# A four-layer graph network on one core: block sums loaded before the last run is stored, counting by quarters, and 32-row products in the update

## The reference

```python
edge_index = jnp.stack([src, dst])                 # 50,000 edges
h = jnp.maximum(_layernorm(x, axis=-1), 0.0)
x = x + _L0_gnn_ref(h, edge_index, edge_weight, w, slw)      # sum at dst
h = jnp.maximum(_layernorm(x, axis=-1), 0.0)
x = x + _L1_gnn_ref(h, edge_index, edge_attr_2, w1)          # sum at src
h = jnp.maximum(_layernorm(x, axis=-1), 0.0)
x = x + _L2_gnn_ref(h, edge_index, edge_attr_8, ...)         # both directions
h = jnp.maximum(_layernorm(x, axis=-1), 0.0)
x = x + _L3_gnn_ref(h, edge_attr_8, node_vec1, ...)
# in _L3_gnn_ref, after agg = segment_sum(m, row):
u = jnp.einsum('ni,nh,ihk->nk', node_features, agg, W_upd_tp) * norm_upd_tp
u = jax.nn.silu(u)
return node_features + (u @ W_upd_lin) * norm_lin
```

## Time and profile before

| what | value |
|---|---|
| times of three runs | 5128.19, 5087.6, 5112.34 us |
| median | 5112.34 us |
| the profiled execution: time, span | 5145.52 us, 5143.8 us |
| mean granted TensorE clock | 0.688 of full speed |
| busy PE, DVE, POOL, ACT | 44%, 54%, 53%, 23% of the span |

### The profile page before, as it was taken

The page is one execution under the profiler, slowest core; times in us unless marked ns, Lnnn a source line. Parts: engine busy times, 40 slices in busy tenths (PEclk is TensorE's granted clock), DMA queues, the critical chain, the costliest instruction groups (busy, mean ns, idle before and its releaser), DMA issues.

```text
span 5143.8 us, 30784 instructions
## 1 busy us (share of the span) xinstructions
PE 2267.1 (44%) x8710; PEld 1601.6 (31%) x8710; DVE 2773.4 (54%) x4101; ACT 1188.9 (23%) x2921; POOL 2750.7 (53%) x2767
## 2 busy tenths in 40 slices
PE   1110036767622100344444226666641455444998
PEld 0000025555511000233333114444431344333444
DVE  8200944545500006355555856767675566565998
ACT  0000012222201102233333323333332223222011
POOL 4777345555577771555555044555523555543787
PEclk6555567878755555677777657777775777777999
DMA  5000112222310012122223412222242222223010
GB/s 148 9 8 8 28 61 84 94 76 94 84 22 22 13 24 84 51 87 80 79 80 81 124 51 77 85 84 85 84 114 79 82 82 82 82 82 92 22 36 29
DMA packets 192782, 345.70 MB, mean 67 GB/s; under 512 B 81018, under 2 KB 159466, under 8 KB 164067
## 3 DMA queue, kind: packets, MB, share of 16 engines
q1 hardware_dynamic: 106128, 290.26, 15.4%
q0 software_dynamic: 81344, 21.38, 5.9%
q10 hardware_dynamic: 5140, 32.09, 1.6%
HBM read 66.26 MB, written 277.24 MB: 67 GB/s over the span
## 4 chain that ended last, share of the span: by engine, by line
another core or an unknown queue 28%; DVE 25%; PE 19%; issue 18%; ACT 3%; POOL 3%; SPq 2%; DMA 1%; DVEq 0%; POOLq 0%
DVE natS L1197 7%; PE psK L570 6%; PE psX L719 4%; PE psK L566 4%; DVE work L1177 3%; PE psX L545 2%; ACT work L829 1%; POOL natD L511 1%; DVE natD L1197 1%; DVE work L1197 1%; DVE h L1087 1%; SPq L430 1%; DVE psX L1084 1%; PE psX L643 1%
## 5 line engine op out<-in xcount | busy, mean ns | idle before, releaser
L487 POOL DMA_INDIRECT rows<-table,rec x1760 | 1666.9, 947 | 1932.5 <-DMA table<-h 508.7
L1197 DVE SCALAR_TENSOR_TENSOR natS<-natS,keep,psK 128x256 f32<-128x256 f32 x1320 | 634.4, 481 | 639.6 <-remote 468.9
L570 PE MATMUL psK<-work 128*128 128x256 f32 x2640 | 787.0, 451 | 425.5 <-issue 196.9
L570 PEld LDWEIGHTS psK<-work 128*128 128x128 f32 x2640 | 595.0, 233 | 576.4 <-issue 385.9
L829 ACT ACTIVATE work<-iota,rec 128x128 f32<-128x128 f32 x1760 | 536.3, 391 | 793.3 <-remote 611.3
L1177 DVE TENSOR_TENSOR work<-at_hi,psX 128x2048 f32<-128x2048 f32 x220 | 502.4, 2284 | 4.2 <-issue 0.4
L469 POOL DMA_INDIRECT edges_by_dst<-natD,pos x391 | 393.3, 1006 | 181.3 <-issue 126.9
L469 POOL DMA_INDIRECT edges_by_src<-natS,pos x391 | 393.1, 1005 | 130.2 <-issue 130.2
L545 PE MATMUL psX<-keep,ident 128*128 128x256 f32 x1080 | 331.9, 431 | 254.3 <-issue 251.0
L566 PE MATMUL psK<-work 128*128 128x128 f32 x1760 | 300.1, 350 | 136.4 <-DVE work L1177 111.0
L719 PE MATMUL psX<-natD,work 128*128 128x512 f32 x784 | 348.3, 596 | 23.6 <-DMA work<-scan_by_column 15.5
(11 more groups left out here) (158 smaller groups left out, 2590.6 us busy)
## 6 DMA issues: line engine op xcount, KB each, us to landing
scan<-natS SPq DMA_DIRECT2D x110, 1024.0 KB
scan_by_column<-natS SPq DMA_DIRECT2D x55, 1024.0 KB
scan<-natD SPq DMA_DIRECT2D x28, 1024.0 KB
rows<-table,rec POOLq DMA_INDIRECT x1760
scan<-work SPq DMA_DIRECT2D x27, 1024.0 KB
table<-h ACTq DMA_DIRECT2D x28, 896.0 KB, 3.6
work<-scan SPq DMA_DIRECT2D x147, 128.0 KB, 2.1
rec<-edges_by_dst SPq DMA_DIRECT2D x110, 84.0 KB
```

The source lines that it names most:

```text
L487: pool.indirect_dma_start(out=rows[k][:, u * D:(u + 1) * D], out_offset=None, in_=table.ap(), in_offset=bass.IndirectOffsetOnAxis(ap=rec[k ...
L570: k = nc.tensor.matmul(psK[:, o:o + BW], lo, spread[par][:, o:o + BW], start=True, stop=True)
L1197: V.scalar_tensor_tensor(acc[par][:, t * BW:(t + 1) * BW], was, keep[s][:, q * G + t:q * G + t + 1], psK[:, t * BW:(t + 1) * BW], ALU.mult ...
```

## The change

There are three edits. First, on SP the loads of the block sums no longer come behind the last `keep_run` of a layer. SP waits for PE's last sum (`summed`) and for the stores of the groups before the last, loads the first chunk, and stores the last group between the first chunk's loads and the second's. Tiles move so that nothing is overwritten: `sq2` goes to `work`, the even accumulator of layer 3 too, and ACT waits for the last two stores before the update. Second, `sort` makes the masks in four quarters of 13, each with its own increment of `in_block`, and `count` waits quarter by quarter; `keys(1)` moves behind the first sort's masks, and `nxt` behind the positions. Third, the update's two products of a step take 32 rows each, those of their two nodes.

```diff
--- before.py
+++ after.py
@@ -180,7 +180,7 @@
         W4 = W1
         uA = prod[:, 0:CW]
         assert nat_at <= NAT * FD, nat_at
-        sq2 = natS[:, 0:CW]
+        sq2 = work[:, 7168:7168 + CW]
         small2 = natS[:, 4096:4096 + 4 * CH]
 
         outer, outerT = prod[:, 1024:1536], prod[:, 1536:2048]
@@ -191,7 +191,8 @@
         tD = natD[:, 2048:2048 + CW]
         halves = [prod[:, i * 512:(i + 1) * 512] for i in range(4)]
 
-        accs = [[prod, work[:, 6144:8192]]] + [[natS[:, i * 2048:(i + 1) * 2048] for i in range(2)]] * 3
+        in_natS = [natS[:, i * 2048:(i + 1) * 2048] for i in range(2)]
+        accs = [[prod, work[:, 6144:8192]], in_natS, in_natS, [work[:, 7168:9216], in_natS[1]]]
 
         psK = ctx.enter_context(nc.psum_tensor("psK", [P, 2048], f32))
         psX = ctx.enter_context(nc.psum_tensor("psX", [P, 2048], f32))
@@ -411,12 +412,12 @@
                         fetch(g + RING)
                         if g:
                             keep_run(g - 1)
-                    for g in range(GROUPS - RING - 1, GROUPS):
-                        keep_run(g)
-                    for g in (GROUPS - 2, GROUPS - 1):
-                        sp.wait_ge(run_out[g % 2], kept_runs(l, g))
-
-                    for c in range(NCH):
+                    def runs_out(g):
+                        for q in (g - 1, g):
+                            sp.wait_ge(run_out[q % 2], kept_runs(l, q))
+
+                    def block_sums(c):
+
                         if l < 3:
                             if c >= 2:
                                 sp.wait_ge(nd[l + 1]["took" if l else "mixed"], c - 1)
@@ -430,6 +431,17 @@
                             t = sp.value_load(last[s][0:1, bass.ds(j + c * PER, 1)], min_val=0, max_val=T - 1)
                             sp.dma_start(to[:, bass.ds(j * BW, BW)], whole.ap()[:, bass.ds(t * BW, BW)])\
                                 .then_inc(signal, 16)
+
+                    for g in range(GROUPS - RING - 1, GROUPS - 1):
+                        keep_run(g)
+
+
+                    sp.wait_ge(e["summed"], GROUPS * G)
+                    for c in range(NCH):
+                        if c == 1:
+                            keep_run(GROUPS - 1)
+                        runs_out(max(GROUPS - 2, (T - 1 - (NB - PER * (c + 1))) // G))
+                        block_sums(c)
 
         @block.gpsimd
         def _(pool):
@@ -520,11 +532,12 @@
 
             def count(s):
 
-                pe.wait_ge(in_block, s + 1)
                 if s:
                     pe.wait_ge(kept, 1)
                 for w, ps in ((allones, psX), (lower, psK)):
                     for b in range(4):
+                        if w is allones:
+                            pe.wait_ge(in_block, 4 * s + (b + 1))
                         for v in range(VS):
                             k = nc.tensor.matmul(v3(ps[:, b * 512:b * 512 + JW], GS), w[:, :],
                                                  OH[:, b * JB:(b + 1) * JB, v * GS:(v + 1) * GS],
@@ -715,7 +728,7 @@
 
                     for j in range(2):
                         b, m = q // 2, 2 * (q % 2) + j
-                        two = slice(0, P)
+                        two = slice(32 * m, 32 * m + 32)
                         k = nc.tensor.matmul(psQ[q % 2][:, j * 512:(j + 1) * 512], sums_in[c % 2][two, b * P:(b + 1) * P],
                                              W4[two, m * 512:(m + 1) * 512], start=True, stop=True)
                     k.then_inc(up["prod"], 1)
@@ -942,6 +955,9 @@
                 if not first:
                     store_out(c - 1)
 
+
+            for g in (GROUPS - 2, GROUPS - 1):
+                act.wait_ge(run_out[g % 2], kept_runs(3, g))
             step(0, True)
             for c in range(1, NCH):
                 step(c, False)
@@ -1009,11 +1025,18 @@
 
             def sort(s):
 
-                for j in range(NBS):
-                    own.did(V.tensor_scalar(OH[:, j, :], keyb[s], float(j), None, ALU.is_equal))
-                own.settle()
-                V.tensor_tensor(OH[:, :, ET:EC], OH[:, :, ET:EC],
-                                padmask[:, None, :].to_broadcast([P, NBS, 2]), ALU.mult).then_inc(in_block, 1)
+                for b in range(4):
+                    own_rows = slice(b * JB, (b + 1) * JB)
+                    for j in range(b * JB, (b + 1) * JB):
+                        own.did(V.tensor_scalar(OH[:, j, :], keyb[s], float(j), None, ALU.is_equal))
+                    own.settle()
+                    V.tensor_tensor(OH[:, own_rows, ET:EC], OH[:, own_rows, ET:EC],
+                                    padmask[:, None, :].to_broadcast([P, JB, 2]), ALU.mult).then_inc(in_block, 1)
+                if s == 0:
+
+                    keys(1)
+                    V.sem_inc(unstaged, 1)
+                    V.sem_inc(copied, 1)
                 A, B, C, I = tiny
                 E4 = before_g.rearrange("p (b j g) -> p b j g", b=4, g=GS)
                 all4 = psX[:, :].rearrange("p (b c) -> p b c", c=512)[:, :, 0:JW]\
@@ -1054,8 +1077,6 @@
                     hit = OH[:, :, v * GS:(v + 1) * GS].rearrange("p (b j) g -> p b j g", b=4)
                     now, nxt = [pre[(v + i) % 2].rearrange("p b (j g) -> p b j g", g=GS) for i in range(2)]
                     own.did(V.tensor_tensor(value.rearrange("p (b j g) -> p b j g", b=4, g=GS), hit, now, ALU.mult))
-                    if v < VS - 1:
-                        own.did(V.tensor_tensor(nxt, hit, now, ALU.add))
                     own.settle()
                     with nc.allow_low_precision(reason="one whole number below 2**24 and zeros"):
                         own.did(V.tensor_reduce(posi[0], value.rearrange("p (j g) -> p g j", g=GS), AX.X, ALU.add))
@@ -1065,6 +1086,9 @@
                     own.settle()
                     V.scalar_tensor_tensor(pos[s][:, v * GS:(v + 1) * GS], posi[1], float(T), posi[2],
                                            ALU.mult, ALU.add).then_inc(places[s], 1)
+                    if v < VS - 1:
+                        own.did(V.tensor_tensor(nxt, hit, now, ALU.add))
+                        own.settle()
 
                 dve.wait_ge(masks, MASKS)
                 dve.wait_ge(firstT, 2 * s + 1)
@@ -1296,9 +1320,6 @@
             dve.wait_ge(cleared, CLEARED)
             dve.wait_ge(ids_in, IDS)
             keys(0)
-            keys(1)
-            V.sem_inc(unstaged, 1)
-            V.sem_inc(copied, 1)
             sort(0)
             sort(1)
             dve.wait_ge(small_in, SMALL)
```

## The result

The changed kernel takes 5054.99 us (median of 9), the kernel before beside it 5119.98 (median of 9): a ratio of 0.988, 95% interval 0.9855 to 0.991. By the ratio that is 60 us less, by the two medians 65. The profiled execution of the changed kernel took 5054.01 us (span 5052.3), close to its median, while that of before, 5145.52, was 25 us over its own; so stages are compared by marks in the two traces, and the whole by the ratio and the medians.

What follows compares the result with a forecast made beforehand. No engine reached 55% busy, so each stage had its own limit. First sort -11.8, second sort -48, block sums -13.5 and 32-row products -24 summed to -97 us: 5112 to 5015, range 4970 to 5085.

Steps and rivals of the forecast that it cites:

- signs of being wrong: First gather staying over 650, or the update's granted clock at 0.6 or less with a chunk over 54 us.
- the pace: While POOL scatters, every engine gets one instruction per about 1.4 us; a product with its weight load takes 2.8.
- The start: First sort: masks in quarters, second keys and `nxt` moved; first scatter near 45.7, -11.8 us.
- The second sort: PE starts after 13 masks instead of 52; -48 us beyond the earlier first scatter, 60 in all.
- The count of products: Second sort: DVE's 156.87 us for the 56 products with `lower` equals 56 x 2.80.
- Rival (E): Second sort: some products run before POOL's scatters fill what paces them; 35 us more gain, 4979 us, chance 0.07.
- The block sums: Between layers and before the update: sooner loads give -3 and -4 behind layers 1 and 2, -6.5 before the update.
- Behind layer 0: Block-sum loads may start 6 to 8 us sooner, but `place(1)` ends no earlier: 0, bounds -6 and +6.
- 32-row products: Update: a step takes 1.13 us, DVE bounds a chunk at 49.8 us instead of 54.41; -24 us.
- I take 4 us off: Update: allowance for PE's clock falling to 1.2 GHz at times, cutting the gain from -28 to -24.
- (D): Update: clock stays at 1.2 GHz throughout, a chunk takes 67.6 us, +92 over seven; 5131 us, chance 0.06.
- The drain between shapes: Update: switching tiling mode drains the array; some 16 switches a chunk at 0.14 us, 2.3 us, sum unchanged.

Runs made afterwards that it cites:

- masks_in_one3: The changed kernel with 128-row update products and each quarter's 13 second-sort masks as one instruction; ratio 0.9846 to the kernel before.
- moves_alone: The kernel before with only `keys(1)` moved behind the first masks and `nxt` behind the positions, no quarters; ratio 0.9968 to the kernel before.
- u64c: The changed kernel with 64-row update products, both products of a step in the same half of the rows; ratio 1.0005 to the kernel before.
- u64_pairs: The changed kernel with 64-row update products, one product of each step in each half of the rows; ratio 0.9824 to the kernel before.
- filler3: The changed kernel with one more, overwritten product of 128 rows and 256 columns in each update step; ratio 1.0306 to the kernel before.
- u128_again: The changed kernel with 128-row update products again, run on chip 5; ratio 0.9937 to the kernel before.

## Why the prediction was partly right

The time of 5054.99 us lies in the range, 40 us over the forecast of 5015 (of which 8 are that the median of before moved from 5112 to 5120). But one of the prediction's own signs of being wrong came true: a granted clock of 0.6 or less in the update with a chunk over 54 us (0.55 and 57.8). And part of the hit is luck: most of the gain hangs on the pace, which three other chips don't show; on one of them the whole change gives 11 us. By its steps:

**The start, -11.8: right.** PE done with `allones` at 25.5 (24.6 forecast), first scatter at 45.70 (45.7).

**The second sort, -48 more: right in mechanism and size where the pace is there.** The long waits end at 279.75 and 436.62 (285 and 440 forecast), the first gather comes at 607.64 (610), 64 us earlier in place of 60. The count of products at 2.80 us holds again to 0.01 us. What the prediction did not know is that the pace is not the kernel's: on three other chips there is none, and the term is then 0. Rival (E), that part of the products runs before the pace sets in, was not what happened to this kernel, but it is what masks_in_one3 showed can happen.

**The block sums, -13.5: right.** -4.2 + 1.7 behind layer 1, -6.1 + 1.1 behind layer 2 (13.74 and 1.56 before, 7.64 and 2.70 after), -6.1 before the update: -13.6 by the traces, and 16 us timed alone.

**Behind layer 0, 0 with bounds of 6: in one trace outside the bounds.** From the last scatter of the second placing to the first gather of layer 1 the kernel before takes 114.4 us and the changed kernel 122.8. But traces with the same code up to there differ as much: with the old order of loads moves_alone has 108.9, with the new one u64c 102.2, masks_in_one3 108.8 and u64_pairs 119.1. So the 8 us are not shown to be a price of the added waits, and I leave the term at 0.

**32-row products, -24: wrong, and this is nearly the whole error.** The step that failed is "I take 4 us off" for the clock, together with the argument against (D) that "a PE without gaps was at 1.00 in this stage, so the state undoes itself". The overlap was right (1.13 us a step) and so was DVE's limit of 49.8 us a chunk, which u64_pairs reached. But with 32 rows the clock fell to 0.55 for the update, and filler3 shows a PE without gaps for 133 us that did not bring it back. (D)'s price was wrong as well: at 1.2 GHz a step of 2.08 us still goes at 1.72, because two steps can run at once in their four row groups, so a chunk costs 57.8 and not 67.6 us. In place of -24 it measured +14 to +19 by the traces from the first product to the end (410.1 and 413.1 against 393.9 to 396.0), and 12 to 15 timed alone.

**The drain between shapes: about as small as estimated.** In u64_pairs a next step starts 1.09 us behind the first of eight small products between two 64-row steps, in the kernel before 0.89 behind, both at the upper clock. That is 0.2 us a piece and, with eight such pieces, some 2 us a chunk, of the order of the prediction's own estimate of 2.3. This fits the rule in the Trainium skill ("TensorEngine Tiling (Array Packing)", Key Properties) that a change of the tiling mode drains TensorE, though no run shows that these 0.2 us are a drain; it decides nothing here.

**The sum.** With what was measured it is -64 - 13.6 + 17 = -61, against -60 by the ratio and -65 by the medians. That it fits to a few us is luck too. The two traces are 64 us apart at the first gather, 52 at the first gather of layer 1, 111 at the update's first product (4749.90 and 4639.24) and 91.5 at the end. From the first to the last, the gathers of layer 1 took 774.5 us in one and 747.4 in the other, with the same code. And moves_alone, only 3 us ahead of the kernel before at the first gather, is 48 us ahead at the update. So with the pace a single execution tells the terms behind the first gather to some tens of us only, and what the waits between the layers are worth is better read from their rows and from the runs on chip 12.

## What to carry to other kernels

In this update splitting the products into row groups paid where the two products at work together cover all the rows: two halves at once gave the short step and kept the clock at 0.96, two quarters at once gave the same step and lost it. Four quarters in one step were not tried. A wait may be measured in instructions and not in work, and then handing work over in parts is worth more than its length says; but look whether another chip shows the same wait before that gain is counted. When DVE instructions are merged to save their number, check what GpSimd's DMAs do while the long ones run.

## What the runs showed of the hardware

- The same program takes 5125 us on one chip and 4047 to 4053 on three others. On the slower one, while POOL issues indirect DMAs, DVE and SP get one instruction per 1.40 us and PE one product with its weight load per 2.80; on the others a run of 13 masks takes 2.7 us and 56 products are done 2.43 us behind the last mask. POOL's own scatters hardly differ: the 391 take 519 us there and 501 to 503 on the others (without the long masks). Most of the difference lies in the layers: from the first to the last the gathers of one take 746 to 785 us there and 549 to 585 on the others. Why the chips differ stays open.
- In the paced stretch PE's rows run ahead of the increments behind them, by 88 us in the kernel before.
- TensorE's clock does not follow the engine's busy share alone. In the update it was 1.00 with 128-row products (busy 98%), 0.96 with two of 64 rows at once (76%), 0.78 with 64 rows one after the other (97%), 0.55 with two of 32 rows at once (94%), 0.65 with these and a filler of 128 rows (98%). The runs show this order and no more exact rule.
- An indirect scatter of 0.96 us takes 5.28 us while a DVE instruction of 5.46 us with two inputs runs. The single masks with one input, in u128_again at the same place, leave it at 0.96, and so do reductions of 2.77 us with one input.
